# A graph network on one core: slots of gathered rows opened three quads ahead instead of six, and quad numbers checked as they are loaded

## The reference

```python
def _gat_layer(x, src, dst, ea, W, We, a_src, a_dst, a_edge, b, n):
    h = x @ W
    e = ea @ We
    s = (h @ a_src)[src] + (h @ a_dst)[dst] + e @ a_edge
    s = leaky_relu(s, 0.2)
    ex = exp(s - segment_max(s, dst)[dst])
    alpha = ex / segment_sum(ex, dst)[dst]
    return segment_sum(h[src] * alpha[:, None], dst) + b

# layer 0, three middle layers mixed with x0 and mid_ws, a last layer; then, on the new rows h:
e = (h[dst] - h[src]) @ theta_w.T + h[src] @ phi_w.T
e = relu(batch_norm(e)); e = relu(batch_norm(e @ fc1_w.T))
x = x + relu(segment_sum(e, dst) / count + h)
```

## Time and profile before

| | |
|---|---|
| runs, us | 17,064.76, 17,099.57, 17,102.23 |
| profiled execution, span, us | 17,111.5 |
| TensorE busy | 59% |
| VectorE busy | 52% |
| ScalarE busy | 37% |
| GpSimd busy | 55% |
| mean granted TensorE clock | 0.745 |
| moved by DMA | 1,019.76 MB |

### The profile page before, as it was taken

One profiled execution on the slowest core, in us unless ns is written; L12 is line 12 of the kernel. 1 busy time (PEld: TensorE's weight loads), 2 busy tenths in 40 slices (PEclk: granted clock), 3 DMA queues, 4 the chain that ended last, 5 costly groups with the idle time before them and its releaser, 6 DMA issues. The chain is left out here.

```text
span 17111.5 us, 305216 instructions
## 1 busy us (share of the span) xinstructions
PE 10174.9 (59%) x64194; PEld 8981.2 (52%) x64195; DVE 8888.7 (52%) x23159; ACT 6297.9 (37%) x12829; POOL 9453.8 (55%) x10337
## 2 busy tenths in 40 slices
PE   5877876555555455556455556455556344444899
PEld 5776766444444444445344455344455344444499
DVE  5555555455555455555455555455556233333777
ACT  2444444333333233334233334233334222222777
POOL 2665554666554666553665554665654555555066
PEclk6667676777777777777677777677777667777999
DMA  3111111111111111111111111211111223333744
GB/s 81 43 43 42 41 42 37 44 43 43 42 42 37 44 43 43 43 42 36 45 44 43 43 42 37 52 44 43 43 43 33 69 85 87 88 88 89 255 142 138
DMA packets 905683, 1019.76 MB, mean 60 GB/s; under 512 B 535591, under 2 KB 589062, under 8 KB 905481
## 3 DMA queue, kind: packets, MB, share of 16 engines
q0 software_dynamic: 300288, 630.00, 14.7%
q1 hardware_dynamic: 517362, 256.23, 6.0%
q10 hardware_dynamic: 87848, 131.57, 2.2%
HBM read 875.68 MB, written 142.21 MB: 59 GB/s over the span
## 5 line engine op out<-in xcount | busy, mean ns | idle before, releaser
L932 POOL DMA_INDIRECT rows<-node_table,idx x9384 | 8883.5, 947 | 6696.0 <-SPq L903 3363.9
L1197 PE MATMUL bank<-rows,work 128*128 x17600 | 3447.2, 356 | 2940.7 <-ACT work L1282 2611.6
L1197 PEld LDWEIGHTS bank<-rows,work 128*128 128x128 f32 x17600 | 3087.8, 262 | 3155.9 <-issue 3151.5
L1263 ACT ACTIVATE work<-bank,v_low 128x512 f32<-128x512 f32 x2200 | 1509.3, 686 | 5713.3 <-remote 3106.9
L1163 PE MATMUL bank<-ident,u_edge 128*128 128x128 f32 x8800 | 2422.3, 353 | 1882.0 <-DVE u_edge L1024 1313.5
L1163 PEld LDWEIGHTS bank<-ident,u_edge 128*128 128x128 f32 x8800 | 1580.3, 180 | 2406.1 <-DVE u_edge L1024 1122.1
L1037 DVE SCALAR_TENSOR_TENSOR work<-bank,acc,work 128x512 f32<-128x512 f32 x1760 | 1321.8, 751 | 2718.4 <-ACT work L1263 1719.1
L1165 PE MATMUL bank<-mask_ident,other_lane 128*128 128x128 bf16 x8800 | 2151.6, 264 | 13.1 <-issue 12.8
L1176 PE MATMUL bank<-ident,work 128*128 128x128 f32 x8800 | 1745.2, 333 | 50.9 <-issue 50.9
L1065 DVE SCALAR_TENSOR_TENSOR acc<-acc,rescale,bank 128x129 f32 x2200 | 767.7, 349 | 1786.1 <-remote 1555.7
L1044 DVE TENSOR_REDUCE group_top<-work 128x1 f32<-128x512 f32 x2200 | 1508.8, 686 | 274.3 <-issue 2.5
(11 more groups left out here) (277 smaller groups left out, 12044.4 us busy)
## 6 DMA issues: line engine op xcount, KB each, us to landing
rows<-edge_features SPq DMA_DIRECT2D x831, 256.0 KB, 2.8
rows<-node_table,idx POOLq DMA_INDIRECT x9384
edge_features<-work ACTq DMA_DIRECT2D x440, 256.0 KB
work<-in_edge_attr SPq DMA_DIRECT2D x48, 256.0 KB
node_table<-acc ACTq DMA_DIRECT2D x147, 65.0 KB
idx<-sources_by_quad SPq DMA_DIRECT2D x150, 32.0 KB
node_table<-hx SPq DMA_DIRECT2D x7, 458.5 KB, 4.0
node_table<-hx SPq DMA_DIRECT2D x1, 3209.5 KB, 19.6
```

The lines of the kernel that those rows point to most:

```text
L932: nc.gpsimd.indirect_dma_start(rows[:, s, q * TW:(q + 1) * TW], None, tables[layer % 2], bass.IndirectOffsetOnAxis(ap=idx[:, half, s, q:q ...
L1197: ins = nc.tensor.matmul(bank[4 + r][:, 0:P + 1], att[:, r, q * P:(q + 1) * P], rows[:, at(slot), q * TW:q * TW + P + 1].rearrange("p a w ...
L1263: nc.scalar.activation(low_side[:, r, :], bank[r][:, :], ACT.Identity, bias=v_low[:, at(now["block"])], scale=ATT_SLOPE).then_inc(low_made, 1)
```

## The change

Three edits. SyncE's `open_slot` moves from six quads ahead of the relay to three. In VectorE's loop over attention groups, and in ScalarE's loop over the groups of the edge-feature stage, the load of a table row no longer gives the reason to skip the check, so that all numbers loaded in it are checked, up to the same bound (`NQ - 1`).

```diff
-        def group_row(eng, r):
+        def group_row(eng, r, waited_against=False):
             _, (quad, slot, block, late_block) = nc.values_load_multi_w_load_instructions(
                 group_rows[0:1, at(r), 0:4].rearrange("a g w -> a (g w)"), engines=(eng.engine,),
-                min_val=0, max_val=NQ - 1, skip_runtime_bounds_check_because=IN_RANGE)
+                min_val=0, max_val=NQ - 1, skip_runtime_bounds_check_because=None if waited_against else IN_RANGE)
...
-        def group_words(eng, r, low, high):
+        def group_words(eng, r, low, high, waited_against=False):
             _, words = nc.values_load_multi_w_load_instructions(
                 group_rows[0:1, at(r), low:high].rearrange("a g w -> a (g w)"), engines=(eng.engine,),
-                min_val=0, max_val=NQ - 1, skip_runtime_bounds_check_because=IN_RANGE)
+                min_val=0, max_val=NQ - 1, skip_runtime_bounds_check_because=None if waited_against else IN_RANGE)
...
-                software_pipeline(sp, NQ, TURN, [(12, load_idx), (0, relay), (6, open_slot)])
+                software_pipeline(sp, NQ, TURN, [(12, load_idx), (0, relay), (3, open_slot)])
...
-                    words = group_words(dve, j + 2, 0, 4 if first else 5)
+                    words = group_words(dve, j + 2, 0, 4 if first else 5, waited_against=True)
...
-                    now["quad"], now["slot"], now["block"], _ = group_row(act, j + 2)
+                    now["quad"], now["slot"], now["block"], _ = group_row(act, j + 2, waited_against=True)
```

## The result

The changed kernel took 18,440.69 us (median of 4 runs, 18,432.15 to 18,457.88). The kernel before, run beside it, took 17,100.90 us (4 runs). The ratio is 1.0789, 95% interval 1.0769 to 1.0809: slower by 1,340 us, where 1,750 was predicted and 18,850 us given as the time.

A forecast was written before the change was run, and what follows sets the result against it. The consumer of gathered rows, not the gather, was taken to set the pace. Terms 1,320 + 264 + 176 = 1,760 us on 17,111, less 12, gave about 18,860, rounded to 18,850 us; range 17,500 to 19,800.

The forecast's parts named there:

- One of its own signs of being wrong: Whole run: forecast called wrong if queue q14's instruction packets rise from 130 to several hundred.
- the layers' length: Attention layers: forecast called wrong if they stay within 100 us of 2,557 us.
- the landing waits: SyncE's waits at L897, 152.9 us before: forecast called wrong if they pass 300 us.
- The price of a pair: Two register instructions per checked word on VectorE and ScalarE: 0.30 us taken, between 0.17 and 0.4 us.
- the estimate of 0.375 us by that rule: VectorE pair by clock rule, 0.96 against 1.2 GHz: 0.3 x 1.25 us, forecast some 330 us higher.
- The step: VectorE's unstalled step between L1037 starts: from 4.35 to 5.85 us, in layer 0 from 4.08 to 5.28 us.
- Half exposed: Half of VectorE's check time paid, the rest in stalls: 1,320 us in layers 1 to 4, 264 us in layer 0.
- rival B: Attention and edge-feature stages: slower consumer shortens gather runs, stalls vanish, kernel faster at 16,440 us; chance 0.06.
- Rival A: Attention layers: checks fall into stalls, layers 1 to 4 each 2,654 against 2,557 us, total 17,490 us; chance 0.15.
- The edge-feature stage: ScalarE's four pairs per group there: one third of 528 us paid, 176 us, with 0 and 528 as ends.
- Slots three ahead: SyncE's openings three relays later in its program: 0 us, with -18 and +100 us as ends.
- Rival C: VectorE's loop of eight groups, 80 instructions longer, fetched anew each turn: adds 770 to 1,540 us; chance 0.08.

## Why the prediction was right, and where it was off

**The forecast as a whole.** It was right in direction and range, with two of its terms too large and one event that it had left out. Part of its closeness is luck: the refetched loop of layer 2 added some 130 us that the sum didn't hold, and without it the growth would have been some 1,210 us against 1,750. One of its own signs of being wrong came true as well: the instruction packets rose from 130 to 430. The others did not (the pair's cost, the layers' length, the landing waits). Layers 1 to 4 take 2,766 to 2,899 us where about 2,890 were said.

**The price of a pair.** 0.28 us from start to start against 0.30 taken; inside 0.17 to 0.4. The first of the pair lasts 183 ns on VectorE and on ScalarE, in the edge-feature stage after (L433 from 15000 to 15200, ns min/median/max), 147 ns:

```profile
L433 ACTq FUSED_REGOPS  x151: 2/147/713, 15000.4 to 15199.9; - x151
```

From pair to pair it is 0.281 us on VectorE and 0.228 us on ScalarE in the median, a factor of 1.23. The Trainium skill, page "Advanced Engine Details and Errata", section Clock Domains, gives 1.2 against 0.96 GHz, a factor of 1.25. The trace agrees. What failed, in the estimate of 0.375 us by that rule, is the 0.3 us of SyncE that I would have multiplied: it was read from starts shown in tenths of a us (0.27 in the trace's own steps), and it ends at another instruction, not at a second pair. The sum by that rule was also wrong: a quarter of 1,320 + 264 is 396 us, not 330.

**The step.** 4.35 us should have become 5.85 and became 5.25 or 5.76 us, by the length of the row's load; the issue gap went from 1.04 to 1.84 and 2.44 us where 2.5 was said. With the long load in both, the step grew by 1.41 us, five times 0.28. Right, except that 4.35 us was the longer of two kinds of step and was taken for all.

**Half exposed.** This share was mis-sized, and it carries most of the difference: the two terms built on it came out 460 us too large together (1,584 against 1,021 + 103). Five pairs are 440 x 5 x 0.28 = 616 us a layer. Layers 1, 3 and 4 grew by 212, 223 and 249 us, 34 to 40%, and layer 0 by 103 of 493 us, 21%. With 0.28 us and a half the four layers would be 1,232 us; they are 1,021, of which some 130 us are the fetching in layer 2 (2,899 against 2,766 and 2,778 beside it). The 62% that I read from the end of layer 4 came from a stretch where many quads have two groups; the lowering to 50% was not enough. On a chip without stalls the share is 2,480 - 2,017 = 463 of 616 us, 75%, and for a single pair 39 of 123 us, 32%. The share isn't a property of the edit but of what bounds the stretch.

**Where the stalls went.** The prediction said that part of the checks falls into stalls that would have been waited out anyway, and that runs of gathers grow shorter. Both came: GpSimd's runs have mostly eight or four calls now, and ScalarE's wait for "remote" fell by 1,413 us. VectorE's own waits show the cover best. Its idle time at L1037 for nothing but its queue grew by 3,000 us, which is about the full price of all pairs (4 x 616 + 493 = 2,957 us), with layer 2's fetching in it, so hardly a pair ran under work of VectorE's own; its "remote" wait at L1065 fell by 1,520 us and its wait at L1037 for ScalarE's L1263 by 400 us (1,925 to 1,525). So at L1065 alone half of the price replaced time in which VectorE had waited for TensorE's product. It is rival B's mechanism at partial strength: the stalls shrank but were not gone, so less than half of the price was paid and the kernel didn't win. Rival A (17,490 us) gave each of layers 1 to 4 97 us more; they grew by over 200.

**The edge-feature stage.** 180 us measured, 176 taken. That is luck: the third was chosen between 0 and 528 us, the pair costs 0.23 us on ScalarE and not 0.30, and no run isolates this term with stalls. Without stalls it is 0, since GpSimd is the bound at 1,950 us.

**Slots three ahead.** 0 taken. L897 waits 183 us now, 153 before. Without stalls two pairs of kernels that differ in it agree: layers 0 and 1 within 1 us, and 1.0030 against 1.0026. With stalls it was tried only together with the checks.

**Rival C.** It got 0.08 and happened in the main loop of one layer of five, for about 130 us in the result and 210 us where no stall covers it, and for three turns at the end of three others. My count of packets was right as a sign and wrong as an argument: that no loop was fetched anew before the change says nothing on one that is longer and lies elsewhere. The Trainium skill, page "Runtime: NRT & Kernel Launch", section Instruction fetch mechanics, gives most engines room for 512 instructions, but as two blocks of 256, and has a taken branch to a block that isn't held wait for a fetch. By that a loop of some 270 fits only where it doesn't reach into a third block, so my "would still fit" left out the half of the rule that mattered. The runs agree with it as far as they go: the same loop is fetched anew in one place and not 40 instructions further on. Where the blocks' borders lie no run shows.

**What I missed.** The whole working rests on one chip's stalls and took them for the kernel's. The sum came out near because the result was measured where stalls were; on the chips without them the same checks cost some 18%, outside the range taken as a ratio (1.02 to 1.16).

## What to carry to other kernels

Register instructions between a load and the first operation that uses it are paid at three quarters of their price and more where that engine is the bound, and at nearly nothing behind an operation of 0.7 us that nothing in between waits for; check there, and only the number that a wait uses (without stalls 18% for all pairs behind the load, 1.7% for one, 0.3% for one behind the operation). A check or any added instruction can also move a loop to where it is fetched every turn: look at the instruction packets by layer, and at one step in a turn that is longer than the rest. Before sizing what stalls will cover, see whether the stalls are there on another chip.

## What the runs showed of the hardware

- **Chips a fifth apart.** The kernel before took 17,100 and 17,293 us on some chips, and 13,690 to 13,708 us on two others. In the traces of changed kernels on those two the same operations take the same time (L1037 751 ns, L932 944 to 947 ns, gathers 1.25 us apart), and no "remote" wait is left. The granted TensorE clock isn't it: the kernel before stalls in layers granted 0.70 to 0.75, and with all checks layers granted 0.71 to 0.73 have no stalls. What the stalls are, why they go with runs of gathers, and why some chips have none, stays open.
- **A loop of some 268 instructions on VectorE** (records between its branches in the trace, 188 before the change) was fetched anew each turn in layer 2 (some 5 packets of 8,192 bytes a turn, one step of about 10 us), and not in layers 1, 3 and 4, nor in layer 2 when it lay 40 instructions further on. In the changed kernel loops of 351 and 397 instructions were fetched anew in three of four places.
- **A register load on VectorE has two lengths.** L443 took 0.59 us in one step and 1.19 us in the next (3449.7 and 3454.9), which makes steps of 5.25 and 5.76 us.
- **An instruction's wait moves forward.** In the kernel with the spread pairs, register instructions put between an operation and one that waits for it took over the wait, and ran behind it themselves (0.82 us idle against 0.15).
- **A register pair costs more than an operation as long.** In layer 4 on a chip with stalls, four pairs (1.12 us a group) added 239 us and one operation of 1.01 us added 26.
